# Quantised cross-attention of a four-layer gated network: keys and values projected in one stage, layer norm, turning and queries in another

## The reference, cut to what matters

```python
q = (x @ Wq + bq).reshape(1, B * N, H, hd)              # x: layer-normalised rows; H = 16, hd = 32
kv = (cond @ Wkv + bkv).reshape(1, -1, 2, H, hd)        # cond: the context, 2048 rows
k, v = (kv[:, :, 0], kv[:, :, 1])
...
q = _fq_sym(q, axis=-1)      # int8 steps per row and head
k = _fq_sym(k, axis=-1)      # the same
v = _fq_sym(v, axis=2)       # steps per head and channel, over all 2048 keys
attn = softmax(q k^T), quantised to 255 steps; out = attn v; out @ Wp + bp
```

## Time and profile before

| | us |
|---|---|
| median of 3 timed runs | 3284.73 (3283.3 to 3286.62) |
| the profiled execution, its own time | 3285.31 |
| its span in the trace | 3283.6 |
| TensorE busy | 2651.4 (81% of the span) |
| VectorE busy | 2482.6 (76%) |
| ScalarE busy | 1907.9 (58%) |
| GpSimd busy | 602.2 (18%) |
| from the first load of Wkv to the first load of the attention | 625.4 to 869.3 |

### The profile page before, as it was taken

One profiled execution on the slowest core, in us unless ns is written; L12 is line 12 of the kernel. 1 busy time (PEld: TensorE's weight loads), 2 busy tenths in 40 slices (PEclk: granted clock), 3 DMA queues, 4 the chain that ended last, 5 costly groups with the idle time before them and its releaser, 6 DMA issues. The chain is left out here.

```text
span 3283.6 us, 61858 instructions
## 1 busy us (share of the span) xinstructions
PE 2651.4 (81%) x21148; PEld 1382.7 (42%) x21148; DVE 2482.6 (76%) x4757; ACT 1907.9 (58%) x2773; POOL 602.2 (18%) x539
## 2 busy tenths in 40 slices
PE   4868999776799999999997779876798747759973
PEld 3444444333365656656564444433211223225542
DVE  5746677565799999999997579825399697985547
ACT  2565433233399999999998255421477434835541
POOL 4441000012101010010101535413012340030013
PEclk8987999897899999999999889987899877869996
DMA  4443421200000000000000110020233010041201
GB/s 152 160 161 102 147 100 47 100 0 16 20 7 14 7 14 7 14 7 7 14 1 13 46 48 1 1 80 13 52 77 78 23 52 1 0 119 37 54 8 54
DMA packets 65346, 152.08 MB, mean 46 GB/s; under 512 B 11840, under 2 KB 20048, under 8 KB 63376
## 3 DMA queue, kind: packets, MB, share of 16 engines
q1 hardware_dynamic: 62368, 140.43, 14.3%
q0 software_dynamic: 2800, 9.18, 0.9%
HBM read 93.61 MB, written 24.38 MB: 36 GB/s over the span
## 5 line engine op out<-in xcount | busy, mean ns | idle before, releaser
L1617 DVE TENSOR_REDUCE s_top<-ps 128x1 f32<-128x512 f32 x1024 | 656.2, 682 | 31.5 <-PE ps L1512 31.2
L1586 ACT ACTIVATE s_prob<-ps,s_shift,m_sq 128x1024 int16<-128x1024 f32 x512 | 614.7, 1201 | 31.4 <-DVE s_shift L1625 31.4
L1512 PE MATMUL ps<-s_ks,s_qs 128*128 128x512 f16 x1024 | 352.8, 386 | 61.8 <-issue 15.3
L1517 PEld LDWEIGHTS ps<-ident,s_prob 128*128 128x128 f16 x4096 | 272.8, 98 | 123.5 <-DVE m_o L1635 51.6
L1517 PE MATMUL ps<-ident,s_prob 128*128 128x128 f16 x4096 | 314.3, 220 | 0.7 <-ACT s_prob L1586 0.5
L1505 PE MATMUL ps<-s_ks,s_qs 128*128 128x512 f16 x1024 | 307.2, 382 | 0.8 <-ACT s_prob L1586 0.5
L1592 ACT ACTIVATE s_probT<-ps 128x1024 f16<-128x1024 int16 x256 | 261.9, 1023 | 7.0 <-PE ps L1517 6.1
L1008 PE MATMUL ps<-m_hT,m_w 128*128 128x512 f16 x1024 | 232.0, 381 | 1.8 <-PEq L105 1.8
L249 PE MATMUL ps<-ident,s_parts 128*128 128x128 f16 x640 | 76.5, 293 | 128.6 <-POOL s_parts L240 126.9
L1630 DVE CAST s_probT<-ps 128x1024 f16<-128x1024 int16 x256 | 174.1, 680 | 4.4 <-PE ps L1517 4.4
L2291 DVE TENSOR_SCALAR s_prob<-ps,s_cap 128x1024 f32<-128x1024 f32 x128 | 158.2, 1269 | 25.3 <-PE ps L2200 25.3
(11 more groups left out here) (407 smaller groups left out, 5596.1 us busy)
## 6 DMA issues: line engine op xcount, KB each, us to landing
s_qs<-m_qT SPq DMA_DIRECT2D x144, 128.0 KB, 2.5
s_ks<-m_kT SPq DMA_DIRECT2D x96, 128.0 KB, 2.4
numbers<-s_numbers SPq DMA_DIRECT2D x21, 512.0 KB, 2.6
s_slabs<-numbers SPq DMA_DIRECT2D x21, 512.0 KB, 5.1
m_ks<-context_parts SPq DMA_DIRECT2D x12, 512.0 KB, 7.5
expert_rows<-s_y SPq DMA_DIRECT2D x19, 256.0 KB, 2.0
s_rows_in<-in_ctx SPq DMA_DIRECT2D x16, 256.0 KB, 2.9
x_sb<-in_L_ffn_W_up SPq DMA_DIRECT2D x4, 1024.0 KB, 7.1
```

The lines of the kernel that those rows point to most:

```text
L1512: pe.matmul(quarter_at(q), qs[:, hb, bass.ds(t * P, P)], ks[:, hb, cols(q, 512)], start=True, stop=True).then_inc(s.top_scored, 1)
L1517: j = pe.transpose(turned(half, F16)[:, cols(m, P)], prob[:, u, cols(8 * half + m, P)].bitcast(F16), k.ident[:])
L1586: act.activation(prob[:, u, cols(half, HALF)], pair(half).rearrange("p m n -> p (m n)"), ACT.Exp, bias=shift[:, u:u + 1], scale=sq[:, bass ...
L1617: dve.tensor_reduce(top4[:, u, q:q + 1], quarter_at(q), AX.X, ALU.max).then_inc(s.top_read, 1)
```

## The change

Two new functions take the place of the six stages.

`quantised_context` does 1, 2 and 3 in one stage. Projection, bias, quantisation and turning of keys keep their instructions. Wkv is loaded as two halves: the half for the keys in four pieces, then the bias, the context, and at last the half for the values in one 1 MB DMA. The low parts of the values' weights are made by GpSimd instead of VectorE. TensorE projects four tiles of keys ahead, then alternates: a tile of keys, a group of values, the turning of an older tile of keys, and at some places half a block of values. Values have three banks for their groups and one for turning. ScalarE's queue takes up keys only when the low parts of the values' weights are there (`w_lo_v`).

`quantised_queries` does 4, 5 and 6 in one stage, tile by tile: VectorE normalises tile t+4 and then quantises the queries of tile t; the copy of the turned x out of PSUM goes from VectorE to ScalarE. Wq comes in one DMA. All loops are written out.

```diff
+def quantised_context(k, cT, w_in, bias, w, kT, values, sv):
+    AHEAD, RING = 4, 3
...
+            for c in range(DC):
+                sp.dma_start(nat[:, 0, c, :], halves[:, 0, c, :]).then_inc(wk_loaded[c], 16)
+            sp.dma_start(bk_bc[:], bias[0:D].partition_broadcast(P)).then_inc(s.bk_loaded, 16)
+            load_context(k, sp, cT)
+            sp.dma_start(nat[:, 1, :, :], halves[:, 1, :, :]).then_inc(s.wv_loaded, 16)
...
+            pe.wait_ge(k.context_first, 16 * k.context_loads)
+            pe.wait_ge(s.w_lo, DC)
+            for t in range(AHEAD):
+                project(t)
+                if t >= 2:
+                    turn(t - 2)
+            pe.wait_ge(k.context_rest, 16 * k.context_loads)
+            pe.wait_ge(s.w_lo_v, DC)
+            for n in range(DC * G):
+                if n + AHEAD < T:
+                    project(n + AHEAD)
+                group(n)
+                if n + AHEAD - 2 < T:
+                    turn(n + AHEAD - 2)
+                if n >= 6 and n % 4 in (2, 3):
+                    turn_values(2 * (n // 4 - 1) + n % 4 - 2)
+            turn_values(2 * DC - 2)
+            turn_values(2 * DC - 1)
...
+        @s.block.vector
...
+            for t in range(T):
+                heads(t)
+                if t >= 8 and t % 4 == 0:
+                    value_numbers(t // 4 - 2)
+            value_numbers(DC - 2)
+            value_numbers(DC - 1)
...
+        @s.block.gpsimd
+        def _(pool):
+            for c in range(DC):
+                pool.wait_ge(s.w_hi_v, c + 1)
+                pool.tensor_tensor(w[:, 1, c, D:2 * D], nat[:, 1, c, :], w[:, 0, c, D:2 * D], ALU.subtract
+                                   ).then_inc(s.w_lo_v, 1)
+            for t in range(T):
+                u = t % 2
+                pool.wait_ge(s.hi_ready, t + 1)
+                pool.tensor_tensor(f16[:, u, 1, :], rows[:, u, :], f16[:, u, 0, :], ALU.subtract).then_inc(s.parts_ready, 1)
...
+        @s.block.scalar
...
+            act.wait_ge(s.wv_loaded, 16)
+            for c in range(DC):
+                act.activation(w[:, 0, c, D:2 * D], nat[:, 1, c, :], ACT.Copy).then_inc(s.w_hi_v, 1)
+            act.wait_ge(s.bv_loaded, 16)
+            act.wait_ge(s.w_lo_v, DC)
+            for t in range(AHEAD - 2):
+                hi(t)
+                if t:
+                    copy_out(t - 1)
+            for n in range(DC * G):
+                t = n + AHEAD - 2
+                if t < T:
+                    hi(t)
+                if t <= T:
+                    copy_out(t - 1)
+                value_bias(n)
+                if n >= 6 and n % 4 in (2, 3):
+                    copy_values(2 * (n // 4 - 1) + n % 4 - 2)
...
+def quantised_queries(k, hT, w_in, bias, scale, w, sq, ints):
+    R = 4
...
+        @s.block.tensor
...
+            turn_h(0)
+            turn_h(1)
+            pe.wait_ge(s.w_lo, DC)
+            for t in range(T + 2):
+                if t + 2 < T:
+                    turn_h(t + 2)
+                if t < T:
+                    project(t)
+                if t >= 2:
+                    turn(t - 2)
...
+        @s.block.scalar
...
+            act.wait_ge(s.w_loaded, 16)
+            for c in range(DC):
+                act.activation(w[:, 0, c, :], nat[:, c, :], ACT.Copy).then_inc(s.w_hi, 1)
+            for t in range(3):
+                hi(t)
+            copy_h(0)
+            copy_h(1)
+            for t in range(T + 2):
+                if t + 3 < T:
+                    hi(t + 3)
+                if t + 2 < T:
+                    copy_h(t + 2)
+                if t >= 2:
+                    copy_out(t - 2)
...
+        @s.block.vector
...
+            for t in range(T):
+                if t + R < T:
+                    normal(t + R)
+                heads(t)
...
-            split_weights(k, k.i.L1_xattn_Wkv, wkv, context=cT)
-            quantised_heads(k, cT, wkv[:, :, :, 0:D], k.i.L1_xattn_bkv[0:D], 1.0, parts=kT, context=True)
-            quantised_values(k, cT, wkv, k.i.L1_xattn_bkv[D:2 * D], values, sv)
+            quantised_context(k, cT, k.i.L1_xattn_Wkv, k.i.L1_xattn_bkv, wkv, kT, values, sv)
...
-            split_weights(k, k.i.L1_xattn_Wq, wq)
-            transposed_parts(k, hT, taken=True)
-            quantised_heads(k, hT, wq, k.i.L1_xattn_bq, scale, sq=sq[:].rearrange("p (h t) -> p t h", t=T), ints=qT)
+            quantised_queries(k, hT, k.i.L1_xattn_Wq, k.i.L1_xattn_bq, scale, wq, sq[:].rearrange("p (h t) -> p t h", t=T), qT)
```

More of the change, by code:

```diff
@@ L1217, in _, with head_steps @@
                 dve.tensor_tensor(out[:, 1, c, :], nat[:, c, :], out[:, 0, c, :], ALU.subtract)
[L1220 to L1227, removed]
+def head_steps(v, rows, amax, step, inv, scaled, scale):
+    v.done(v.engine.tensor_reduce(amax, rows.rearrange("p (h d) -> p h d", d=HD), AX.X, ALU.max,
+                                  apply_absolute_value=True))
+    v.done(v.engine.tensor_scalar(step, amax, scale / 127.0, 1e-8, ALU.mult, ALU.max))
+    v.done(v.engine.reciprocal(inv, step))
+    if scale != 1.0:
+        v.done(v.engine.tensor_scalar(inv, inv, scale, None, ALU.mult))
+    v.done(v.engine.tensor_tensor(scaled.rearrange("p (h d) -> p h d", d=HD), rows.rearrange("p (h d) -> p h d", d=HD),
+                                  inv.unsqueeze(2).broadcast_to([P, H, HD]), ALU.mult))
@@ L1240, in _, with turn_h @@
         @s.block.tensor
         def _(pe):
[L1242 to L1244 removed]
+            def turn_h(t):
+                pe.wait_ge(s.h_parts, t + 1)
+                if t >= R:
+                    pe.wait_ge(s.h_copied, t - R + 1)
+                for m in range(2 * DC):
+                    i = pe.transpose(k.ps16[:, 4 + t % R, cols(m, P)], hparts[:, t % R, m // DC, cols(m % DC, P)], k.ident[:])
+                i.then_inc(s.h_turned, 1)
@@ L1265, in _, with turn @@
[L1265 to L1275, removed]
+            def turn(t):
+                pe.wait_ge(s.numbers_ready, t + 1)
+                if t >= 2:
+                    pe.wait_ge(s.copied, t - 1)
+                for c in range(DC):
+                    i = pe.transpose(k.ps16[:, 2 + t % 2, cols(c, P)], numbers[:, t % 2, cols(c, P)], k.ident[:])
+                i.then_inc(s.turned, 1)
@@ L1279, in _ @@
             v = Steps(dve, s.vsteps)
-            dve.wait_ge(s.bias_loaded, 16)
[L1281 to L1337, removed]
-                                   ACT.Copy).then_inc(s.copied, 1)
-                else:
-                    act.activation(out[:, :, :, bass.ds(t * P, P)],
-                                   k.ps16[:, 2 + u, :].rearrange("p (l c n) -> p l c n", l=2, c=DC),
-                                   ACT.Copy).then_inc(s.copied, 1)
-            hi(0, 0)
[L1346 to L1349, removed]
-            hi(T - 1, 1)
-            copy_out(T - 2, 0)
-            copy_out(T - 1, 1)
```

231 lines of the change are left out of this document (162 added, 69 removed).

## The result

The changed kernel takes 3249.8 us (median of 4 runs, 3246.9 to 3251.6) against 3284.0 for the kernel before (4 runs): a ratio of 0.9901, 95% interval 0.9885 to 0.9916. Its profiled execution took 3251.6, with a span of 3249.9, 33.7 us less than before. Forecast for that execution were 3254.2. One execution in this document, the second of e11's six, was slow (3385.0 us, granted clock 0.79 against 0.91 in the other five) and is left out of that kernel's median.

What follows compares the result with a forecast made beforehand. No engine was full over the stretch; VectorE bound the keys and queries, TensorE the values. Gains of 19.0 (context) and 12.1 (queries) sum to 31.1, taking 3285.3 to 3254.2 us, median 3254; range 3245 to 3270.

Steps and rivals of the forecast that it cites:

- the second rival: Query stage without collision loss (-4.8) and TensorE's clock not falling in its pause (-2.5): 3247 us; chance 0.14.
- Context, start: Merged keys and values: 1 MB of context lands at 634.8 us, three tiles projected by 644.9, loop restarts, first turn and tile done by 659.0.
- The pause: Context stage: TensorE idles 7.7 us until the values' weights are split and GpSimd's first keys' low part is done at 652.6.
- Context, steady: Context stage: TensorE is the bound at 5.59 us an iteration, last group out at 739.3; VectorE keeps up by 1.5.
- Queries, start: Merged query stage: first projection done 18.1 us after the stage's start, against 41.7 before, gaining 23.6 us.
- Queries, pace: Query stage: VectorE stays the bound at 3.47 us a tile, plus 0.56 normalising and 0.40 collision for 12 tiles.
- The collision's 0.40: Query stage: GpSimd beside the quantisation costs VectorE 0.40 us a tile, as in the keys; bounds nothing and 1.15.
- VectorE becomes the bound through GpSimd: Each low part stops VectorE for 1.15 us as phase drifts: queries 9.0 more, keys 4.5 more, 3268 us; chance 0.16.
- Less collision, quicker starts: No collision loss in the queries (-4.8), no clock fall in TensorE's pause (-2.5): 3247 us; chance 0.14.
- The lower clock: TensorE stays at 1.2 GHz: in queries alone 3285 us, chance 0.04; in both merged stages 3364 us, chance 0.03.
- The chains do not interleave: One in-order stream holds TensorE some 2 us in every iteration, 24 of the gain gone: 3278 us; chance 0.04.
- the first rival: GpSimd's low parts each stop VectorE for a whole 1.15 us, making it the bound: 3268 us; chance 0.16.

Runs made afterwards that it cites:

- e11: Changed kernel with context-stage loads in order of need and GpSimd's low part of x in phase in the query stage; 3231.8 us, ratio 0.9854.
- e10: Changed kernel with context-stage loads in order of need: keys' weights, 1 MB of context, both biases, values' weights, 3 MB of context; 3239.4 us, ratio 0.9864.
- e8: Changed kernel with the values' half of the weights loaded before the 3 MB part of the context instead of after it; 3244.0 us, ratio 0.9880.
- e3: Changed kernel with the merged context stage kept, but all keys first and then all groups of values; 3267.7 us, ratio 0.9948.
- e5: Changed kernel with four matmuls instead of twelve for a group of values (high parts alone, less exact); 3236.6 us, one run.
- e4: Kernel before with VectorE's loop over pairs of tiles in the keys' and queries' stages written out, nothing else; 3280.6 us, ratio 0.9993.
- e6: Changed kernel with GpSimd's low part of x left out in the query stage, its place in the waits kept; 3247.5 us, ratio 0.9884.
- e7: Changed kernel with GpSimd's low part of tile t waiting until VectorE has normalised tile t+1 in the query stage; 3250.5 us, ratio 0.9896.
- e1: Kernel before with the merged stage of keys and values alone, query stages left as three; 3262.3 us, ratio 0.9940.
- e9: Changed kernel run once more, unaltered, as the measure on the same chip; 3246.2 us, ratio 0.9887.

## Why the prediction was right, point by point

**The total.** Forecast 3254.2 for the profiled execution, measured 3251.6; a gain of 31.1 against 33.7. It lies in the forecast's own range. The halves were off in opposite ways: context 19.0 forecast and 16.8 measured, queries 12.1 and 17.9. That the total came so near is therefore partly luck, and the median of 3249.8 is nearer to the 3247 of the second rival than to 3254. What bears the forecast out is the stages and their rows, not the total.

**Context, start.** TensorE was to begin 9.4 us after the first load and began after 11.5: the step that failed is "0.75 MB less at 340 GB/s, so it lands at 634.8". The size was right, the rate was not. The window 626.9 to 638.4 moved 255 GB/s, that is 2.9 MB; the same stretch before, from 625.4 to the landing at 637.0, moved 320 GB/s, 3.7 MB. In both, 0.57 MB more had moved than the loads up to the 1 MB part hold (2.25 and 3 times 2^20 bytes), so the loads behind took no larger share than before. At 320 GB/s the 2.9 MB would have taken 9.2 us. The engines were nearly as busy (0.87 against 0.92) and moved less: the stage's loads made 3858 packets where 2802 carried the same 6.57 MB before. The weights now come in half rows; whether this is the cause was not tried. The 256 KB of bias ahead is not the whole of it, since e10, without it there, had 249 GB/s up to its first matmul. Over the runs the time to the first matmul was between 9.5 and 12.5 us. The pause was forecast at 7.7 and was 8.3, both its ends being late (by 2.3 and 2.9 us), with its cause: shown by e8, which moved the load and took half of it. What I had not seen is that GpSimd's four operations stop VectorE's second tile too (L1334 above, 1.26).

**Context, steady.** 80.3 us forecast from the loop's start to the last group's bias (659.0 to 739.3), 81.7 measured (662.05 to 743.76), TensorE dense, VectorE with time to spare. e3 and e5 show both halves of the claim. The end was 11.2 where 11.9 was forecast.

**Queries, start.** 18.1 forecast, 17.1 measured.

**Queries, pace.** 4.43 a tile was forecast (3.47 + 0.56 + 0.40) and 4.14 measured. The step that failed is "loops written out I cost at nothing": e4 shows 0.18 a tile on VectorE, 2.9 of the 5.7 us by which the stage was misjudged. The evidence that I used, the values' stage, was TensorE's stream and says nothing of VectorE's loop. Half of the cost could have been read in the trace before, as neighbouring additions in a pair and across pairs lie 3.40 and 3.56 apart; the other half, the later copy, only e4 shows. The normalising was 0.45, by start to start, not 0.56: 1.3 us more; the quicker start gave 1.0. The collision's 0.40 was right, taken over from the keys, and e6 and e7 show it; it came in 11 tiles, not 12.

**The rivals.** *VectorE becomes the bound through GpSimd*: no. In the queries the collision repeated at 0.40, for the phase does not drift; it locks, since ScalarE's and GpSimd's work starts from VectorE's own instruction. *Less collision, quicker starts*: it did not come by itself, but e7 and e8 make it. *The lower clock*, in one stage or both: no; both steady windows have 1.00. The transposes beside the matmuls did not hold it down, and it fell in the pause and came back within one tile, which took 4.0 us (5.2 in e1 and e9). *The chains do not interleave*: no, TensorE lost 0.5 us in 82.

## What to carry to other kernels

Two stages with different bounds gained here by alternating their work in one stream; joining them without alternating gained nothing. The query stage gained in another way, by an earlier start. The sum for such a stage is the fuller engine's own work, plus the way in and out, and the way in is where to look next: what the in-order queues wait for first, and in which order the loads land. Where GpSimd and VectorE share a tile's work, look for an instruction of VectorE's that ends with GpSimd's; when GpSimd's operation is itself started by VectorE's work, the collision repeats in every tile, and what helped here was to start that operation under instructions of VectorE that do not mind it. Writing out VectorE's loop gained 0.18 us a tile in one stage and nothing in the other, so its cost has to be looked for between the instructions of the stage at hand.

## What the runs showed of the hardware that I had not expected

- VectorE is stopped by a GpSimd operation on SBUF not only in its tensor-with-scalar instructions (0.17 to 0.57) but in those with two inputs in SBUF: L1229 and L1338 took 1.30 and 1.52 us instead of 0.69. The additions with one input in PSUM (0.69) and the maxima (0.69) were untouched in e7. The Trainium skill ("SBUF — State Buffer", the two sides and the shared port pair) has this rule for instructions with two SBUF inputs; the first rival rested on it, and the rows of e10 agree.
- TensorE's clock: in e10 the tile after a pause of 3.07 us took 4.44 us, in e11 after 2.17 us it took 2.75. In both the eight transposes right after the pause still ran at the upper level of 2.4 GHz (0.62 us, against 1.03 at the lower in the changed kernel). Only behind them did e10's granted clock fall, to 0.50 from 651.2 to 653.7, while e11's stayed at 1.00. With the same code, a shorter pause kept the upper level and a longer one did not.
- VectorE's loop over pairs of tiles cost 0.18 us a tile in the queries (e4), about half at a copy whose place depends on the counter and half at the loop's turn, and nothing visible in the keys, whose last instruction is longer (0.69 against 0.43) and which have no such copy.
